# A gated state-space layer with experts: who adds the turned halves of the state, and how far behind the query follows

## The reference, cut to what matters

```python
def step(Sc, inp):
    a11, a12, bt, k, v = inp
    S0, S1 = (Sc[..., 0], Sc[..., 1])
    r0 = a11[..., None] * S0 + a12[..., None] * S1
    r1 = -a12[..., None] * S0 + a11[..., None] * S1
    Sr = jnp.stack([r0, r1], -1)
    err = v - jnp.sum(k * Sr, -1)
    Sn = Sr + bt[..., None, None] * err[..., None] * k
    return (Sn, Sn)
...
y = jnp.sum(Q * Y, -1)
```

## Time and profile before

| what | value |
|---|---|
| median of 3 runs | 1750.14 us (1748.82 to 1751.21) |
| profiled execution, its own time | 1749.82 us |
| its span | 1747.9 us |
| PE busy | 1346.1 us, 77% |
| DVE busy | 1260.0 us, 72% |
| ACT busy | 384.0 us, 22% |
| POOL busy | 67.9 us, 4%, 28 sums of 2.42 us on the mean, all in the first pass |
| second pass of sample 0 | from 427.5 us (L1208) to 621.9 us (last L461) |
| second pass of sample 1 | from 1206.7 us to 1400.6 us |

### The profile page before, as it was taken

The page is one execution under the profiler, slowest core; times in us unless marked ns, Lnnn a source line. Parts: engine busy times, 40 slices in busy tenths (PEclk is TensorE's granted clock), DMA queues, the critical chain, the costliest instruction groups (busy, mean ns, idle before and its releaser), DMA issues. The chain is left out here.

```text
span 1747.9 us, 12480 instructions
## 1 busy us (share of the span) xinstructions
PE 1346.1 (77%) x4304; PEld 772.8 (44%) x4304; DVE 1260.0 (72%) x1841; ACT 384.0 (22%) x610; POOL 67.9 (4%) x32
## 2 busy tenths in 40 slices
PE   3980877714888886796799999597988886899995
PEld 1440222212444454543455555364544455566663
DVE  3869999998999957486938999986999957000002
ACT  2421000000002043342421111133010143332333
POOL 0000112110000000000001211100000000000000
PEclk9995766656999988598899999899999997799997
DMA  3000110011111022100113222124111000222221
GB/s 133 1 7 0 49 48 36 25 75 46 36 37 48 13 101 97 55 0 6 48 53 105 72 73 73 50 71 169 39 46 49 20 29 1 79 85 72 73 84 48
DMA packets 51103, 93.85 MB, mean 54 GB/s; under 512 B 4577, under 2 KB 39777, under 8 KB 50018
## 3 DMA queue, kind: packets, MB, share of 16 engines
q1 hardware_dynamic: 51042, 93.06, 15.2%
HBM read 73.12 MB, written 19.92 MB: 53 GB/s over the span
## 5 line engine op out<-in xcount | busy, mean ns | idle before, releaser
L476 PE MATMUL ps<-wshare,uT 128*128 128x512 f32 x512 | 244.9, 634 | 55.3 <-DVE kz L1205 55.2
L568 PE MATMUL ps<-kz 128*128 128x256 f32 x1024 | 243.1, 381 | 29.2 <-ACT kz L745 29.2
L556 PE MATMUL ps<-kz 128*128 128x512 f32 x512 | 245.7, 603 | 6.7 <-DMA kz<-in_w 6.1
L568 PEld LDWEIGHTS ps<-kz 128*128 128x128 f32 x1024 | 195.5, 191 | 110.2 <-issue 59.0
L476 PEld LDWEIGHTS ps<-wshare,uT 128*128 128x128 f32 x512 | 101.6, 204 | 178.7 <-issue 118.1
L1358 DVE TENSOR_TENSOR kz<-kz,b_s 128x256 f32<-128x256 f32 x32 | 13.0, 411 | 228.8 <-ACT kz L729 228.7
L745 ACT ACTIVATE kz<-ps,small 128x512 f32<-128x512 f32 x128 | 87.9, 687 | 393.8 <-PE ps L556 393.7
L426 PE MATMUL ps<-wshare,xnT 128*128 128x512 f32 x256 | 154.9, 736 | 13.2 <-DVE wshare L1068 13.2
L556 PEld LDWEIGHTS ps<-kz 128*128 128x128 f32 x512 | 97.2, 193 | 89.3 <-issue 82.6
L409 PE MATMUL ps<-ident,uT 128*128 128x128 f32 x256 | 44.9, 306 | 83.6 <-DVE work L1083 58.0
L785 POOL TENSOR_TENSOR work<-work 128x1024 f32<-128x1024 f32 x28 | 67.7, 2418 | 1051.3 <-DVE work L1110 1051.3
(11 more groups left out here) (239 smaller groups left out, 1879.4 us busy)
## 6 DMA issues: line engine op xcount, KB each, us to landing
kz<-in_w SPq DMA_DIRECT2D x128, 256.0 KB, 2.9
kap_d<-kz SPq DMA_DIRECT2D x26, 512.0 KB, 2.6
kz<-kap_d SPq DMA_DIRECT2D x26, 512.0 KB, 3.2
uT<-in_x SPq DMA_DIRECT2D x8, 512.0 KB, 5.7
wshare<-in_wq SPq DMA_DIRECT2D x2, 2048.0 KB, 7.6
kz<-in_x SPq DMA_DIRECT2D x2, 2048.0 KB, 12.7
coef<-in_x SPq DMA_DIRECT2D x2, 2048.0 KB, 8.4
wshare<-in_wk SPq DMA_DIRECT2D x2, 1024.0 KB, 11.5
```

The source lines that it names most:

```text
L476: t = mm(ps[:, 2 * (j % 2) + c, :], uT3[:, k, j * P:(j + 1) * P], wq_s[:, k, c, :], start=(k == 0), stop=(k == KI - 1))
L556: t = mm(ps[:, 4 + i % 2, :], w1_r[r][:, k, (f % 2) * P:(f % 2 + 1) * P], x2T[:, k, n * 512:(n + 1) * 512], start=(k == 0), stop=(k == KM ...
L568: t = mm(ps[:, 6 + q // 2, (q % 2) * DM:(q % 2 + 1) * DM], hbuf(i)[:, q * P:(q + 1) * P], w2_r[r][:, f % 2, :], start=(f == 0 and q % 2 == ...
```

## The change

`turned` leaves DVE. POOL adds the two halves of X and writes the sum into `k2(j)`, and `query` then multiplies there in place. DVE's `e` instruction of token j raises `turn_ready`, which releases POOL's sum for token j-1 (by then both turns of j-1 are done); POOL raises `turned_ready`. `query(j-2)` in place of `query(j-1)` runs in token j, so the query follows two tokens behind. The order on DVE becomes: sr, sr, turn 0 of j-1, Y, turn 1 of j-1, e, `value(j+1)`, `query(j-2)`, subtraction, Y, st. `vh` gets a second buffer. The statistics run after tokens 7, 11, 15 and at the end. At the end both turns of token 15 are followed by `query(14)` and `query(15)`. PE, ACT and SP keep their programs.

```diff
--- before.py
+++ after.py
@@ -164,6 +164,8 @@
         x_ready = sem("x_ready")
         z1_ready = sem("z1_ready")
         sum_ready = sem("sum_ready")
+        turn_ready = sem("turn_ready")
+        turned_ready = sem("turned_ready")
         out_stored = sem("out_stored")
         xc_ready = sem("xc_ready")
         xt_ready = sem("xt_ready")
@@ -783,6 +785,10 @@
                     if i >= 2:
                         pool.wait_ge(sum_ready, b * (L - 2) + i - 1)
                     nc.gpsimd.tensor_tensor(PSt[:, :, 2], PSt[:, :, 2], Z, ALU.add).then_inc(sum_ready, 1)
+                X = tmp[:, 2048:4096].rearrange("p (a i n) -> p a i n", a=2, i=2)
+                for j in range(L):
+                    pool.wait_ge(turn_ready, b * L + j + 1)
+                    nc.gpsimd.tensor_tensor(k2(j), X[:, :, 0], X[:, :, 1], ALU.add).then_inc(turned_ready, 1)
 
 
         @block.vector
@@ -1181,34 +1187,33 @@
                 st = work[:, 0:1024].rearrange("p (i n) -> p i n", i=2)
                 sr = work[:, 1024:2048].rearrange("p (i n) -> p i n", i=2)
                 Y = tmp[:, 0:1024].rearrange("p (i n) -> p i n", i=2)
-                e, vh = tmp[:, 1024:1536], tmp[:, 1536:2048]
+                e = tmp[:, 1024:1536]
+                vh = [tmp[:, 1536:2048], tmp[:, 4096:4608]]
                 X = tmp[:, 2048:4096].rearrange("p (a i n) -> p a i n", a=2, i=2)
                 at = {}
 
                 def value(j):
                     dve.wait_ge(ut_ready, 2 * L * b + L + j + 1)
-                    if j >= 1:
-                        after(at["e"])
-                    tt(by_head(vh, 0), by_head(ps[:, 4 + j % 2, :], 0), wide(cf[:, CV, j]), MUL).then_inc(ut_used, 1)
+                    if j >= 2:
+                        after(at["s"][j % 2])
+                    tt(by_head(vh[j % 2], 0), by_head(ps[:, 4 + j % 2, :], 0), wide(cf[:, CV, j]), MUL).then_inc(ut_used, 1)
 
                 def turn(j, i):
                     after(at["st"])
-                    at["o"] = mark(tt(by_head(X[:, i], 1), by_head(st, 1), wide(cf[:, H_ + 2 * i:H_ + 2 * i + 2, j]), MUL))
-
-                def turned(j):
-                    after(at["o"])
-                    at["o"] = mark(tt(X[:, :, 0], X[:, :, 0], X[:, :, 1], ADD))
+                    if i == 0 and j >= 1:
+                        dve.wait_ge(turned_ready, b * L + j)
+                    at["t"] = mark(tt(by_head(X[:, i], 1), by_head(st, 1), wide(cf[:, H_ + 2 * i:H_ + 2 * i + 2, j]), MUL))
 
                 def query(j):
-                    after(at["o"])
+                    dve.wait_ge(turned_ready, b * L + j + 1)
                     dve.wait_ge(kq_ready, 2 * L * b + L + j + 1)
-                    tt(k2(j), X[:, :, 0], ps[:, 2 * (j % 2):2 * (j % 2) + 2, :], MUL).then_inc(kq_used, 1)
+                    tt(k2(j), k2(j), ps[:, 2 * (j % 2):2 * (j % 2) + 2, :], MUL).then_inc(kq_used, 1)
 
                 dve.wait_ge(start_ready, b + 1)
                 v.tensor_copy(st, ps[:, 6:8, :]).then_inc(start_used, 1)
                 value(0)
                 dve.wait_ge(start_used, b + 1)
-                at["st"] = n_chain[0]
+                at["st"], at["s"] = n_chain[0], {}
                 for j in range(L):
                     k = k2(j)
                     after(at["st"])
@@ -1222,26 +1227,30 @@
                     at["y"] = mark(tt(Y, k, sr, MUL))
                     if j >= 1:
                         turn(j - 1, 1)
-                    after(at["y"])
-                    at["e"] = mark(tt(e, Y[:, 0], Y[:, 1], ADD))
+                        after(at["y"])
+                        tt(e, Y[:, 0], Y[:, 1], ADD).then_inc(turn_ready, 1)
+                    else:
+                        after(at["y"])
+                        at["e"] = mark(tt(e, Y[:, 0], Y[:, 1], ADD))
+                    if j + 1 < L:
+                        value(j + 1)
+                    if j >= 2:
+                        query(j - 2)
                     if j >= 1:
-                        turned(j - 1)
-                    after(at["e"])
+                        dve.wait_ge(turn_ready, b * L + j)
+                    else:
+                        after(at["e"])
                     dve.wait_ge(ut_used, 2 * L * b + L + j + 1)
-                    at["e"] = mark(tt(e, vh, e, SUB))
-                    if j >= 1:
-                        query(j - 1)
+                    at["e"] = at["s"][j % 2] = mark(tt(e, vh[j % 2], e, SUB))
                     after(at["e"])
                     at["y"] = mark(tt(Y, k, e.unsqueeze(1).to_broadcast([P, 2, DI]), MUL))
                     after(at["y"])
                     at["st"] = mark(tt(st, sr, Y, ADD))
-                    if j + 1 < L:
-                        value(j + 1)
-                    if j % 4 == 2 and j > 4:
+                    if j % 4 == 3 and j > 4:
                         group_stats(b, j // 4 - 1)
                 turn(L - 1, 0)
-                turn(L - 1, 1)
-                turned(L - 1)
+                tt(by_head(X[:, 1], 1), by_head(st, 1), wide(cf[:, H_ + 2:H_ + 4, L - 1]), MUL).then_inc(turn_ready, 1)
+                query(L - 2)
                 query(L - 1)
                 dve.wait_ge(kq_used, 2 * L * b + 2 * L)
                 group_stats(b, NCH - 1)
```

## The result

| | before | after |
|---|---|---|
| median | 1750.29 us (4 runs, 1748.82 to 1751.21) | 1778.32 us (4 runs, 1773.26 to 1782.33) |
| profiled execution, its span | 1749.82, 1747.9 us | 1773.26, 1771.4 us |

The ratio is 1.0159, 95% interval [1.013, 1.0189], that is 28 us. The forecast was 1766 us with a range up to 1778, so the measured median lies just beyond its end. The direction was right; the forecast size was 16 us, and 28 were measured. The profiled execution is the fastest of the four, 5 us under their median, so the trace shows a little less than the whole loss.

A forecast was written before the change was run, and what follows sets the result against it. DVE was taken to bound the second pass, with PE only 1.7 us slack per token. The new loop and pass end gave +10.7 us for two samples, the clock +5.5: +16.2 on 1749.82, forecast 1766 us, range 1752 to 1778.

The forecast's parts named there:

- The end of the pass: From just behind `e` of token 14 to the last PE turn: 30.17 us before, 32.73 after, +2.56 per sample.
- The new wait: On DVE, `value(j+1)`, now ahead of `query(j-2)`, waits for PE's transposes of token j+1; about 1.1 us in most tokens.
- loop of one round: Second pass: query's end, PE's 9.35 us, handover, `value`, `query` follow each other in one round, 11.31 us in sum.
- The lock: POOL's sum and DVE's two-SBUF-input subtraction don't run side by side: 0.70 us lost, hidden where `value` is late.
- handover to POOL: From the end of DVE's releasing instruction to the start of POOL's sum: 0.15 us.
- DVE's round: DVE's time per second-pass token: 11.07 us before; after, 10.16 alone and 10.86 with POOL's sum holding the subtraction.
- First query group behind the long pause of 15 us: PE's first bank-waiting query products, after query(0) in token 2: 9.55 us in place of 7.13, +2.42.
- V(1) to V(14): Second pass, from just behind `e` of token 1 to that of token 14: 149.71 us before, 152.50 after, +2.79.
- clock term: PE's query groups after the 3.71 us pauses behind mid-pass statistics slow by 1.38 us each, four times: +5.5 us.
- +10.7 us forecast: Both samples' second passes without the clock, +5.35 us per sample.
- Rival 3: PE's clock stays down: each of 9 looped rounds takes +2.2 us, 40 us added, 1806 us; chance 6%.
- 3.7 us pause: PE's pause after mid-pass statistics, 13.06 - 9.35 = 3.71 us, expected to slow the next query group.

The follow-up runs named there:

- kernel with filler: The changed kernel with three extra, unread 256-column products per token on PE (from token 4) in its pause ahead of the query products: 1762.19 us, ratio 1.0074.
- half-sum kernel: The changed kernel with POOL adding only one of the two components (512 columns), the other left out: 1777.87 us, ratio 1.0150.
- padded one: The kernel before with one extra, unread 128-column DVE sum per token in the second pass (from token 1): 1758.16 us in one execution.
- kernel with `value` back: The changed kernel with `value(j+1)` put back behind the state's sum at the token's end: 1762.76 us, ratio 1.0073.

## Why the prediction was wrong

The end of the pass, which answers to the earlier trace rows, first and last row of the changed kernel:

```profile
1392.24 0.69 DVE L1199 TENSOR_TENSOR work<-ps,coef 128x512 f32<-128x512 f32 x1 [1.00 <-PE ps L411]
...
1423.14 1.95 PE L463 MATMUL ps<-ident,kz 128*128 128x128 f32 x16
```

**Right, with its numbers.** The new wait is at `value` for the transposes, in a loop of one round: 11.31 forecast, 11.27 measured. The lock: subtraction held 0.70 forecast, 0.65 measured (the handover to POOL is 0.08 us here and not 0.15); DVE's round 10.86, measured 10.82. The end of the pass: 32.73 forecast, 32.85 measured, from 1392.24 to 1425.09 (before 30.17). First query group behind the long pause of 15 us: 9.55 taken, 10.16 and 10.14 measured. V(1) to V(14) without the clock: 152.50, and 152.41 in the kernel with filler. That kernel, at 1762.2, is the forecast without its clock term (+10.7 us forecast, +12.4 measured). (The prediction calls V(j) the moment 0.60 us behind the start of `e`; its sums count to the start of `value`, as I do here, and in the looped rounds that is about 1 us later.) The rule of the Trainium skill that I went by, in "SBUF — State Buffer" (Who interferes with whom), that a VectorE instruction with two SBUF inputs contends with a GpSimd instruction that reads SBUF, holds here: 1.33 against 0.68 us with and without the overlap. The note of the Trainium skill in "Advanced Engine Details and Errata" (VectorE Performance Modes, Mode Summary), which names the two-port modes alone, does not cover this case.

**The term that was mis-sized** is the clock. I charged 5.5 us, for the four groups behind statistics, because one group after a pause of 2.15 us ran at full clock, and took from it that the 1.9 us pauses of the ordinary rounds are safe. One row was too little: in that place PE had paused 1.51 us before it and 2.15 only once, and the changed kernel pauses 1.91 in every round. Rival 3 named this (the clock low in each looped round), at 2.2 us in 9 of 9 rounds and 6%; what came is 1.70 us in 7 of 12 groups. In the profiled execution two of the seven fall together with statistics and cost nothing of their own, and no `value` waits behind the last one (token 14). Four of 1.70 are left: V(1) to V(14) is 159.21, where the forecast with its clock term has 155.26. That is 13.6 us for both passes in this fastest execution. By the medians, filling the pause gives 16.1 us back, where 5.5 stood in the forecast; with the forecast's own 10.7 that is 26.8 of the measured 28.

**Statistics.** In the profiled execution the slow groups fell on the rounds with statistics (516.54 to 529.51 is 12.97, where the forecast has 13.06 for DVE alone), so each covers the other, and there is no 3.7 us pause. In the execution of the half-sum kernel shown above they did not fall together, and groups of 10.1 us follow pauses of 3.62. I take this to be the spread of the changed kernel's runs (9 us, where the kernel before has 2.4); with one profiled execution per kernel that is argued and not shown.

**Open.** What length of pause in what length of round lets the clock fall: here pauses of 1.48 and 1.71 us did not. Behind a pause of 1.91 the group was slow in 14 of 24 cases in the changed kernel, behind 1.92 in 4 of 8 in the padded one, and behind 1.95 in 5 of 9 in the kernel with `value` back, so about every second time in each. Single pauses of 1.93, 2.15 and up to 2.38 behind shorter ones did not do it. The runs don't separate the pause from its share of the round.

## What to carry to other kernels

When a consumer is moved ahead in one engine's order, follow what it waits for around the other engine: here a wait that had two rounds of room was left with one, and the loop of both engines became longer than either engine's own round. In such a loop every loss of the slower partner is paid at once, the clock's too; an engine that pauses a little in each round is not a safe partner, and moving one independent step ahead in its queue repairs it. A sum moved to POOL was worth here only what DVE could do beside it with one SBUF input; collect such instructions (PSUM readers, statistics) behind the release.

## What was unexpected of the hardware

- PE's clock falls in rounds with a pause of only 1.91 us in 11.27 (granted 1.00 in one round, 0.87 in the next), and 1.3 us of useless products per round keep every query group of tokens 3 to 14 at 7.13 us, its time at full clock: 16 us in all.
- POOL released while a DVE instruction with two SBUF inputs runs (`e`, 0.68 us) shows a sum of 2.74 us in place of 2.35, but is done 0.21 us earlier than when released by that instruction's end (2.90 against 3.11 behind its start).
- A statistics instruction on DVE (one SBUF input) ran beside POOL's sum at 0.69 us, its time alone.
